# A gated block on one core: expert transfers from the slot loop on, and a new token preparation

## What is computed

```
x   = x + tanh(g_xattn) * cross_attention_and_ff(layernorm(x))
y   = layernorm(x)
o   = slot_query + mha(slot_query, y, y, d_W*, d_b*)             # 16 slots per batch, 16 heads of 32
h   = layernorm(o) * e_ln_g[slot] + e_ln_b[slot]
u,g = silu(h @ e_W1[slot] + e_b1[slot]), silu(h @ e_Wg[slot] + e_bg[slot])  # 512 -> 2048
o   = o + (u * g) @ e_W2[slot] + e_b2[slot]                      # each slot has its own expert
out = x + tanh(g_ffn) * mha(y, o, o, c_W*, c_b*)
```

## Time and profile before

| what | value |
|---|---|
| median of 3 runs | 2633.45 us (2632.62 to 2637.53) |
| the profiled execution | 2635.73 us |
| its span, first to last instruction | 2633.7 us |
| busy: TensorE, VectorE, ScalarE, GpSimd | 2307.1, 977.8, 630.3, 389.9 us |
| moved over the span | 467.23 MB, mean 177 GB/s |
| mean granted TensorE clock | 0.928 of 2.4 GHz |

### The profile page before, as it was taken

How to read it: one execution, slowest core, us unless ns; L and a number is a source line. 1 busy time by engine, 2 the same in 40 slices (tenths; PEclk the granted TensorE clock), 3 DMA queues, 4 the chain that set the end, 5 groups by cost and what they waited for, 6 DMA issues and landing times. The chain is left out here.

```text
span 2633.7 us, 29521 instructions
## 1 busy us (share of the span) xinstructions
PE 2307.1 (88%) x11361; PEld 1691.2 (64%) x11361; DVE 977.8 (37%) x1581; ACT 630.3 (24%) x973; POOL 389.9 (15%) x239
## 2 busy tenths in 40 slices
PE   6999999998799999999999999978885555555897
PEld 5677777776688888888888888857651111111476
DVE  7666656654222222222222233335510000001577
ACT  2554444554211111111111111123300000000221
POOL 5443334423000000000000000002200000000022
PEclk9999999999899999999999999989967777777898
DMA  4122221111433333333333533235459999999165
GB/s 156 57 85 85 86 85 54 46 57 58 173 140 139 139 140 140 139 139 140 140 139 139 192 128 127 96 120 191 175 227 414 413 413 420 417 418 350 56 255 207
DMA packets 134340, 467.23 MB, mean 177 GB/s; under 512 B 10531, under 2 KB 12099, under 8 KB 115798
## 3 DMA queue, kind: packets, MB, share of 16 engines
q1 hardware_dynamic: 132390, 465.92, 46.5%
q10 hardware_dynamic: 1872, 0.27, 0.1%
HBM read 382.01 MB, written 84.15 MB: 177 GB/s over the span
## 5 line engine op out<-in xcount | busy, mean ns | idle before, releaser
L1215 DVE TENSOR_TENSOR u<-ff_sig,ff_a 128x512 f32<-128x512 f32 x128 | 88.0, 688 | 452.0 <-ACT ff_sig L1177 452.0
L1177 ACT ACTIVATE ff_sig<-ff_gate 128x512 f32<-128x512 f32 x128 | 76.5, 598 | 744.4 <-PE ff_a L1137 744.4
L1137 PE MATMUL ff_gate<-ff_nT_hi,w_hi 128*128 128x512 f32 x512 | 200.0, 391 | 15.3 <-DMA ff_nT_lo<-xnT 15.3
L1137 PE MATMUL ff_gate<-ff_nT_lo,w_hi 128*128 128x512 f32 x512 | 199.9, 390 | 0.0
L1137 PE MATMUL ff_gate<-ff_nT_hi,w_lo 128*128 128x512 f32 x512 | 199.8, 390 | 0.0
L1137 PE MATMUL ff_a<-ff_nT_hi,w_lo 128*128 128x512 f32 x512 | 199.2, 389 | 0.0
L1137 PE MATMUL ff_a<-ff_nT_lo,w_hi 128*128 128x512 f32 x512 | 199.2, 389 | 0.0
L1151 PE MATMUL ff_down<-w_hi,u_hi 128*128 128x512 f32 x512 | 199.2, 389 | 0.0
L1151 PE MATMUL ff_down<-w_lo,u_hi 128*128 128x512 f32 x512 | 199.2, 389 | 0.0
L1151 PE MATMUL ff_down<-w_hi,u_lo 128*128 128x512 f32 x512 | 199.2, 389 | 0.0
L1137 PE MATMUL ff_a<-ff_nT_hi,w_hi 128*128 128x512 f32 x512 | 199.2, 389 | 0.0
(11 more groups left out here) (353 smaller groups left out, 4563.0 us busy)
## 6 DMA issues: line engine op xcount, KB each, us to landing
e_w<-in_L_ffn_e_W SPq DMA_DIRECT2D x32, 4096.0 KB, 23.5
e_wg<-in_L_ffn_e_Wg SPq DMA_DIRECT2D x16, 4096.0 KB, 28.0
ff_nT_hi<-xnT SPq DMA_DIRECT2D x32, 1024.0 KB, 4.8
ff_nT_lo<-xnT SPq DMA_DIRECT2D x32, 1024.0 KB, 6.8
ff_x<-x SPq DMA_DIRECT2D x32, 1024.0 KB, 8.0
x<-ff_x SPq DMA_DIRECT2D x32, 1024.0 KB, 4.4
ff_raw<-in_L_xattn_Wff SPq DMA_DIRECT2D x36, 256.0 KB, 5.7
xnT<-nT_hi SPq DMA_DIRECT2D x8, 1024.0 KB, 5.1
```

What stands on the lines that cost most here:

```text
L1137: last = nc.tensor.matmul(UP[f % 2][g][:, :], w, m_, start=c == 0, stop=c == 3 * KT - 1)
L1177: nc.scalar.activation(sig[:, f % 2, :], UP[f % 2][1][:, :], ACT.Silu).then_inc(sig_ready, 1)
L1215: nc.vector.tensor_tensor(u32[:, f % 2, :], sig[:, f % 2, :], UP[f % 2][0][:, :], ALU.mult).then_inc(u_ready, 1)
```

## The change

- Slot stage: the bias and slot-query part of the output product is made in the prelude and kept in `o1`. The value product comes out turned: `wv` is the loaded operand, four heads in four groups of 32 output partitions, and its bias is added on VectorE. The layer norm folds gain and shift into two `scalar_tensor_tensor` operations, the first beside the square root. TensorE also writes `o2T`, the turned sum of `o1` and `e_b2`, which stays in SBUF to the end.
- Transfers: SP loads gains, shifts and `e_b2` in the first iteration of the slot loop, a quarter of expert 1's W2 in each of the iterations 1 to 4, and W1, Wg and W2 of expert 0 at the loop's end, each when its place is free. From expert 2 on, W2 is begun by ScalarE. W2 comes in runs of 8 KB per partition instead of 2 KB; rows are picked with a stride to match. The bias rows lie in Wg's buffer of expert 1, so that this load waits for them.
- The result of an expert is folded in turned form and added to `o2T` on VectorE; the stores into `y_d` are gone.
- Token stage: preparation and batches are one block. Keys stay dense (`kT`) and are multiplied 32 rows at a time, the four heads of a 128-row group into four banks; `v_diag` has 64 columns per 128-row group, with the heads' own rows picked by a mask. The order is `wq`, keys, values, `bias_k`, `WK`, `VW`, and then the first batch's scores; the second batch's loads wait for the preparation's last unit.

```diff
+        with ExitStack() as after_prelude:
+            over = Memory(nc, after_prelude, whole)
+            e_gain, e_shift, h_in, o1 = (over.sbuf(n, [P, D]) for n in ("e_gain", "e_shift", "h_in", "o1"))
+            oT = over.sbuf("oT_s", [P, KT, P])
+            b2 = over.sbuf("e_b2_rows", [E, D])
...
-                for b in range(B):
-                    sp.dma_start(e_gain[b * NS:(b + 1) * NS, :], I["L0_ffn_e_ln_g"]).then_inc(gains_in, 16)
-                    sp.dma_start(e_shift[b * NS:(b + 1) * NS, :], I["L0_ffn_e_ln_b"]).then_inc(gains_in, 16)
...
+                nc.tensor.matmul(G[2][:, :], ones[0:1, :], bias["o"][:, :], start=True, stop=False)
+                nc.tensor.matmul(G[2][:, :], every[:, :], sq[:, :], start=False, stop=True).then_inc(pe_step, 1)
...
+                dve.wait_ge(pe_step, KT + 5)
+                nc.vector.tensor_copy(o1[:, :], G[2][:, :])
...
-                with sp.Fori(0, B - 1) as b:
+                for b in range(B - 1):
                     sp.wait_ge(y_ready, b + 1)
                     sp.dma_start(xin[:, :, :], of(x_v, b + 1)).then_inc(x_in, 16)
+                    if b == 0:
+                        sp.dma_start(b2[:, :], I["L0_ffn_e_b2"]).then_inc(gains_in, 16)
+                        for n in range(B):
+                            sp.dma_start(e_gain[n * NS:(n + 1) * NS, :], I["L0_ffn_e_ln_g"]).then_inc(gains_in, 16)
+                            sp.dma_start(e_shift[n * NS:(n + 1) * NS, :], I["L0_ffn_e_ln_b"]).then_inc(gains_in, 16)
                     keep(b)
+                    if 1 <= b <= 4:
+                        load_w2_part(sp, second_w2, I["L0_ffn_e_W2"][1], b - 1, w2_in[1])
                 keep(B - 1)
                 sp.wait_ge(yn_lo_done, B)
                 sp.wait_ge(scored, B * 2)
-                load_w1(sp, first_w1, I["L0_ffn_e_W1"][0], first_w1_in)
+                load_w1(sp, first_w1, I["L0_ffn_e_W1"][0], w1_in[0])
+                sp.wait_ge(g_ready, B * PER + U_Z + 2)
+                load_w1(sp, first_wg, I["L0_ffn_e_Wg"][0], wg_in[0])
                 sp.wait_ge(yT_out, B * 32)
+                sp.wait_ge(g_ready, (B + 1) * PER)
+                load_w2(sp, first_w2, I["L0_ffn_e_W2"][0], w2_in[0])
...
+        pe2, dve2, act2 = (mem.sem(f"d2_{n}") for n in ("pe", "dve", "act"))
+        with nc.Block() as block:
+            @block.tensor
+            def _(pe):
...
+                for c in range(KT):
                    for k in range(KT):
+                        for g in range(4):
+                            h = c * 4 + g
+                            last = nc.tensor.matmul(G[0][g * SD:(g + 1) * SD, c * P:(c + 1) * P], wv[:, k, h * SD:(h + 1) * SD],
+                                                    zT[:, k, h, :, :].rearrange("p b s -> p (b s)"), start=k == 0, stop=k == KT - 1)
+                last.then_inc(pe2, 1)
...
+                pe.wait_ge(dve2, 2)
+                pe.wait_ge(gains_in, (2 * B + 1) * 16)
+                for k in range(KT):
+                    nc.tensor.matmul(G[1][:, k * P:(k + 1) * P], o1[:, k * P:(k + 1) * P], ident[:, :], start=True, stop=False)
+                    last = nc.tensor.matmul(G[1][:, k * P:(k + 1) * P], b2[:, k * P:(k + 1) * P], every[:, :], start=False, stop=True)
+                last.then_inc(pe2, 1)
...
+            @block.scalar
+            def _(act):
+                nc.scalar.preload_act_table_set("sqrt_and_others")
+                act.wait_ge(dve2, 3)
+                nc.scalar.activation(sd[:, :], sd[:, :], ACT.Sqrt).then_inc(act2, 1)
+                act.wait_ge(pe2, 3)
+                nc.scalar.copy(o2T[:, :, :].rearrange("p k n -> p (k n)"), G[1][:, :])
...
+                nc.vector.tensor_tensor(oT[:, :, :], G[0][:, :].rearrange("p (k n) -> p k n", k=KT),
+                                        bv_col[:, :].unsqueeze(2).to_broadcast([P, KT, P]), ALU.add).then_inc(dve2, 1)
+                dve.wait_ge(pe2, 2)
+                nc.vector.tensor_tensor(o1[:, :], G[2][:, :], o1[:, :], ALU.add).then_inc(dve2, 1)
...
+                nc.vector.scalar_tensor_tensor(h_in[:, :], o1[:, :], mv[:, 0:1], e_gain[:, :], ALU.subtract, ALU.mult)
+                dve.wait_ge(act2, 1)
+                nc.vector.reciprocal(sd[:, :], sd[:, :])
+                nc.vector.drain()
+                nc.vector.scalar_tensor_tensor(h_in[:, :], h_in[:, :], sd[:, 0:1], e_shift[:, :], ALU.mult, ALU.add).then_inc(dve2, 1)
...
+def load_w2(queue, w2, src, arrival):
+
+    queue.dma_start(w2[:, :, :].rearrange("p (q j) n -> p q (j n)", q=4),
+                    src.rearrange("(q p j) n -> p q (j n)", q=4, p=P)).then_inc(arrival, 16)
+
+
+def load_w2_part(queue, w2, src, q, arrival):
+
+    J = FF // 4 // P
+    queue.dma_start(w2[:, q * J:(q + 1) * J, :].rearrange("p j n -> p (j n)"),
+                    src[q * J * P:(q + 1) * J * P, :].rearrange("(p j) n -> p (j n)", p=P)).then_inc(arrival, 16)
 
...
-        block_at = [q * C + j * P for j in range(J) for q in range(Q)]
+        block_at = [slice(q * C + j, (q + 1) * C, J) for j in range(J) for q in range(Q)]
...
-            sp.dma_start(w2[i][:, :, :], of(I["L0_ffn_e_W2"], e).rearrange("(f p) n -> p f n", p=P)).then_inc(w2_in[i], 16)
...
-                load(sp, 1, 1, 0)
+                load_w1(sp, w1[1], I["L0_ffn_e_W1"][1], w1_in[1])
+                sp.wait_ge(bias_turned, 2)
+                load_w1(sp, wg[1], I["L0_ffn_e_Wg"][1], wg_in[1])
                 with sp.Fori(1, E // 2) as turn:
                     for i in range(2):
-                        load(sp, turn * 2 + i, i, turn)
-                        store(turn * 2 + (i - 2))
-                store(E - 2)
+                        e = turn * 2 + i
+                        sp.wait_ge(u_ready, turn * 2 + (i - 1))
+                        load_w1(sp, w1[i], of(I["L0_ffn_e_W1"], e), w1_in[i])
+                        sp.wait_ge(g_ready, turn * 2 + (i - 1))
+                        load_w1(sp, wg[i], of(I["L0_ffn_e_Wg"], e), wg_in[i])
...
-                for b in range(B):
-                    sp.dma_start(lent[b * NS:(b + 1) * NS, 3, 3, :], I["L0_ffn_e_b2"]).then_inc(b2_in, 16)
-                store(E - 1)
...
-                    nc.tensor.matmul(YS[0:B, :], fold[:, :], y_parts[:, :], start=True, stop=True).then_inc(folded, 1)
+                    for k in range(KT):
+                        last = nc.tensor.matmul(YS[:, k * B:(k + 1) * B], y_parts[:, k * P:(k + 1) * P], fold[:, :], start=True, stop=True)
+                    last.then_inc(folded, 1)
...
-                    act.wait_ge(y_out, e * 16)
+                    act.wait_ge(folded, e)
...
+                    if not isinstance(e, int):
+                        load_w2(act, w2[i], of(I["L0_ffn_e_W2"], e + 2), w2_in[i])
...
-                    nc.vector.tensor_copy(ys, YS[0:B, :]).then_inc(y_done, 1)
+                    slots = o2T[:, :, :].rearrange("p k (b e) -> p (k b) e", e=E)
+                    to = slots[:, :, e:e + 1] if isinstance(e, int) else slots[:, :, bass.ds(e, 1)]
+                    nc.vector.tensor_tensor(to, to, YS[:, 0:KT * B].unsqueeze(2), ALU.add).then_inc(y_done, 1)
...
+        spare = [*TB, *OB]
+        U_WQ, U_K, U_V, U_BK = 0, KT, KT + 1, KT + 2
+        U_WK = U_BK + CH
+        U_VW = U_WK + KT * CH
+        U_END = U_VW + B * HT
+        every_bank = [*spare, *SC]
+        bank_at = [(u - U_BK) % 8 if U_BK <= u < U_VW else u % len(spare) for u in range(U_END)]
+        of_bank = lambda u: every_bank[bank_at[u]]
+        hi_count = lambda u: u - U_WK + 1
+
+        of_heads = lambda bank: bank[:, :].rearrange("p (c b s) -> p c b s", c=KT, b=B)
+        to_heads = lambda t, g: t.rearrange("p b (c g s) -> p g c b s", c=KT, g=CH)[:, g]
+
+        def wk_place(u):
+            k, g = divmod(u - U_WK, CH)
+            return [to_heads(t[:, k, :, :], g) for t in WK]
+
+        def vw_place(u):
+            b, t = divmod(u - U_VW, HT)
+            return [x[:, b, t, :] for x in VW]
...
+                for n in "kqv":
+                    sp.dma_start(bias[n][:, :], I[f"L0_ffn_c_b{n}"].rearrange("(k p) -> p k", p=P), allow_slow_non_contiguous=True).then_inc(c_small_in, 16)
+                sp.dma_start(bo_gate[:, :], I["L0_ffn_c_bo"].unsqueeze(0).to_broadcast([P, D])).then_inc(c_small_in, 16)
+                load_y(0, 0)
+                load_x(0, 0)
+                sp.wait_ge(w_ready, U_END)
...
+                pe.wait_ge(c_weights_in, 48)
+                for u, w in ((U_K, wk), (U_V, wv)):
+                    bank = claim(u)
+                    for c in range(KT):
+                        for k in range(KT):
+                            last = nc.tensor.matmul(bank[:, c * P:(c + 1) * P], w[:, k, c * P:(c + 1) * P], o2T[:, k, :],
+                                                    start=k == 0, stop=k == KT - 1)
+                    last.then_inc(w_ready, 1)
+                pe.wait_ge(w_free, U_K + 1)
+                banks = [claim(U_BK + g) for g in range(CH)]
+                for c in range(KT):
```

(54 more changed lines are left out.)

350 lines of the change are left out of this document (101 added, 249 removed).

## The result

The changed kernel takes 2565.9 us (median of 4 runs, 2564.6 to 2567.9) where the kernel before took 2633.66 beside it (4 runs, 2632.62 to 2637.53): a ratio of 0.9741, 95% interval 0.9724 to 0.9758. That is 67.7 us less. The forecast was 2555, its range 2543 to 2578; the sum of its terms was 78.3. The profiled execution took 2567.9 us, with a span of 2566.1.

The account below looks back on a forecast made before the run. It took the experts' stage to wait for memory, with chains of small dependent steps on both sides; savings of 25.1 + 17.3 + 1.7 + 4.0 + 30.2 = 78.3 us off the 2633.45 median gave 2555 us, range 2543 to 2578.

Parts of the forecast that it names:

- Last slot block, 27.5 saved: Slot stage's last block, 48.9 us: turned value product at 8, Wo product 6.1, less norm and copying; 21.4 left, 27.5 saved.
- Rival (B): Narrow tiles don't run side by side, or the clock stays at 1.2 GHz: 2569 to 2575 us; chance 0.13.
- Prelude, 2.4 lost: Slot prelude: moved matmuls and a copy, 4.4 us, replace some 2.0 us of splitting at its end; 2.4 us lost.
- 3.7 leave for the prelude: Last slot block: bias and slot-query matmuls, 3.7 us, move out of it into the prelude.
- Slot loop, the quarters of W2 and the late yT store, 0: Slot loop: W2 quarters (2.5 us each) have 10 us of cover; store goes 3.3 later; nothing, up to 1 us if late.
- Rival (D): Early W2 quarters delay the slot loop by 2.5 us each, or expert 0 waits for its weights: 2565 us; chance 0.05.
- e_g of expert 1 comes 24.8 after the block's start: Experts' start: expert 1's gate product comes 24.8 us after the block's start, 24.9 before, leaving a stream hole of some 2.
- Stream, 17.3 with 1.7: Experts' stage: weights between Wg 1 and Wg 15 take 407.2 us against 424.5, 17.3 saved; 1.7 more after e_g of 15.
- I take half of it: Stream's end: expert 15's W2 may land with or after Wg 15; half is counted, so 13.5 W2 at 9.96 us.
- the four token weights follow Wg 15 at once and land with or before the block: End of the experts' stage: token weights load straight behind Wg 15, landing by the token block's start.
- Transition and token preparation, 34.2: Last fold to first score: next block's delay 4.3 becomes 0.3, 4.0 saved; token preparation 76.2 becomes 46, 30.2 saved.
- Batches, "unchanged": Token batches after the preparation: 127 us, unchanged.

Follow-up runs that it names:

- prelude_back_late: w2_1_late with the products of Wo's bias and the slot-query rows moved back from the prelude into the last slot block; 2570.93 us, ratio 0.9770.
- value_old: The changed kernel with only the turned value product undone (old product, copy, four turns, copy with bias); 2589.91 us, ratio 0.9834.
- w2_1_late: The changed kernel with expert 1's W2 loaded in the experts' stage behind its Wg, not in quarters in the slot loop; 2576.28 us, ratio 0.9775.
- bias_first: The changed kernel with the expert biases turned before expert 0's up product instead of behind it; 2558.55 us, ratio 0.9725.
- w2_on_sp: The changed kernel with W2 of experts 2 to 15 issued from SP's queue again, ahead of the token weights, packets still 8 KB; 2555.27 us, ratio 0.9714.
- x1_behind: The changed kernel with x of batch 1 loaded behind y of batch 2 instead of ahead of it; 2556.37 us, ratio 0.9734.

## Why the prediction came out as it did

The forecast was in its range and 10.9 us too low. Its large terms were right in mechanism; what it missed lies beside them.

- Last slot block, 27.5 saved: 29.1 and the 1.0 or 2.0 us (by the clock) of the bias products ahead of it, some 30.6. The value product was taken at 8 and measured 5.31 (3.70 in prelude_back_late, at full clock), the Wo product at 6.1 and measured 3.70, both since I priced the block at its old clock; the earlier trace rows shows 0.50 for the value product alone, and the rest of the old block stood at 0.59. value_old gives the product and its turn 24 to 25 us, against 19.5 + 1.9 by my steps without the bias. Rival (B) falls: narrow tiles ran side by side in both places.
- Prelude, 2.4 lost: 2.5 at half clock (w2_1_late against prelude_back_late), so the term held; this profile shows 5.7, of which 3.2 are the clock of unchanged products. What failed is the other end: "3.7 leave for the prelude" was worth 1.0 in the block as it is now.
- Slot loop, the quarters of W2 and the late yT store, 0: the loop takes 149.2 us, and 149.7 to 150.9 before with 1.0 or 2.0 us of bias products in it. VectorE waited 1.92 us for x once, in the first iteration, and the loop took no longer by it; the two kernels without the quarters in the loop took 148.6 and 149.8. Right. Rival (D) falls.
- "e_g of expert 1 comes 24.8 after the block's start": e_u to e_g takes 27.2 for 23.4. The bias turns took 4.0 and e_u 6.5, and Wg of 1 was issued 15.4 us after the first bias load where I had 12.6. The hole that I put at 2 us and priced at nothing costs 4.0 by bias_first's trace. A hole in a stream that binds the stage is a term of the sum, and I had left it out.
- Stream, 17.3 with 1.7: 16.0 of 19.0. The sizes held (9.96 us for an 8 KB W2, forecast and by the 421 GB/s). The step that failed is "I take half of it" for W2 of 15, with "the four token weights follow Wg 15 at once and land with or before the block": I let them go first at no cost. They took 9.8 us of the stream ahead of the last W2. Strict order gives back 5.6 us by the trace and 7.1 by the time (w2_on_sp). That W2 of 15 comes last, which the Trainium skill's rule on turns (DMA: Bandwidth & Descriptors, Queues, rings and completion order) would have had as a gain of 5 us, came true and was no gain, because a third transfer was in the way.
- Transition and token preparation, 34.2: 35.4. K and V took 7.3 and not 10.0, at full clock; WK ran at a granted clock of 0.50 (2405 to 2420), bound by VectorE's halves, about as forecast. VW had the whole factor of two, 0.86 us for each of its later units of four products, at a clock of 1.00.
- Batches, "unchanged": 130.1 for 124.8 to 127.1. What failed is that I looked at the second batch's late loads only for who waits for them, and nobody does. Their landing sets when GpSimd works, and that holds VectorE. The holds account for part of the 4 us (5 us more of them than before, and 2.7 of 4.1 in x1_behind); the rest is open, and profiles of one code differ by 2 to 4 us here.

The table's rows miss the 78.3 by 12.3 us: 3.7 in the stretch with the hole, 3.0 by the stream, 4.1 by the batches, 5.4 by start and prelude (mostly these profiles' own), less 2.7 more of gain in slot loop and last block and 1.2 in the token stage. 1.6 of the 12.3 is the second profile of before being shorter. The errors have both signs: without the 3.9 us of gain that were not forecast, the time would have been that much higher, still in the range.

## What to carry to other kernels

Where the DMA share was 1.0, time was bytes over rate, and three things counted: the size of packets, holes at the stream's start, and what stood ahead of the last transfer that was due; waits of TensorE inside it, here 185 us, said nothing. A second queue gave no rate but took away the order: the transfer with the small packets came late, and this cost time at the end, where it was the last one needed. Before moving small products or loads off a chain, price them at the clock and in the idle gaps that the chain will have afterwards, and ask which engine a late load sets to work beside whom.

## What the runs showed that was not expected

- One VectorE product with both operands in SBUF took 4.80 us instead of 0.69 when it began 0.24 us after a GpSimd product of 4.49 us. Those with an operand in PSUM that are shown above did not slow. The two lines with both operands in SBUF have it in their means (against 690 ns), in the groups by form of the kernel before from 2506 on, of the changed kernel from 2436 on, and of x1_behind from 2427 on:

```profile
L2243 DVE TENSOR_TENSOR c_prob<-c_prob,c_top 128x512 f32<-128x512 f32 x16 | 18.1, 1131 | 1.2
L2252 DVE TENSOR_TENSOR c_prob<-c_prob,c_total 128x512 f32<-128x512 f32 x16 | 14.6, 910 | 1.2
```

```profile
L2207 DVE TENSOR_TENSOR c_prob<-c_prob,c_top 128x512 f32<-128x512 f32 x16 | 19.0, 1190 | 1.2
L2216 DVE TENSOR_TENSOR c_prob<-c_prob,c_total 128x512 f32<-128x512 f32 x16 | 18.7, 1171 | 1.6 <-issue 0.5
```

```profile
L2207 DVE TENSOR_TENSOR c_prob<-c_prob,c_top 128x512 f32<-128x512 f32 x16 | 20.3, 1270 | 1.2
L2216 DVE TENSOR_TENSOR c_prob<-c_prob,c_total 128x512 f32<-128x512 f32 x16 | 14.8, 922 | 1.6 <-issue 0.5
```

  So 16 x (0.500 + 0.481) = 15.7 us of VectorE's time in the changed kernel's batches are such holds, 10.6 in the kernel before and 13.0 in x1_behind: they are not new, the change made them longer. What moving GpSimd's product elsewhere would bring was not tried.
- Rates with the DMA engines full: 432 GB/s at 32 KB packets, 421 at 8 KB, 385 at 2 KB (the first and last worked out above).
- Between profiles of the same code the start of the slot prelude lay anywhere in 1737.3 to 1742.4, and the prelude in 22.7 to 28.6 by the granted clock.
